# A four-layer kernel on one core: the bias wait, the projection's PSUM bank, the split of the maxima, and identity products at two places

## The reference

```python
x = x + _layernorm(_L0_attn_ref(_layernorm(x), Wqkv, bqkv, Wout, bout))
x = x + _layernorm(_L0_ffn_ref(_layernorm(x), ...))    # two-level Kronecker experts, top 2 of 64
x = x + _layernorm(_L1_attn_ref(_layernorm(x), ...))   # gated state-space layer
x = x + _layernorm(_L1_ffn_ref(_layernorm(x), ...))    # soft mixture of 64 experts, 32 slots each
```

```python
scores = einsum('bhid,bhjd->bhij', q, k) * scale
band = abs(idx[:, None] - idx[None, :]) <= 64
attn = softmax(where(band, scores, neg), axis=-1)
out = einsum('bhij,bhjd->bhid', attn, v).reshape(b, n, d) @ Wout + bout
```

## Time and profile before

| | us |
|---|---|
| median of 3 runs | 841.96 (840.02 to 847.08) |
| the profiled execution | 849.46 |
| its span in the trace | 847.4 |
| PE busy | 665.3 (79%) |
| DVE busy | 488.3 (58%) |
| ACT busy | 362.7 (43%) |
| POOL busy | 332.2 (39%) |
| PE clock granted, mean | 0.889 |

### The profile page before, as it was taken

One profiled execution on the slowest core, in us unless ns is written; L12 is line 12 of the kernel. 1 busy time (PEld: TensorE's weight loads), 2 busy tenths in 40 slices (PEclk: granted clock), 3 DMA queues, 4 the chain that ended last, 5 costly groups with the idle time before them and its releaser, 6 DMA issues. The chain is left out here.

```text
span 847.4 us, 17741 instructions
## 1 busy us (share of the span) xinstructions
PE 665.3 (79%) x7348; PEld 380.4 (45%) x7348; DVE 488.3 (58%) x1088; ACT 362.7 (43%) x626; POOL 332.2 (39%) x324
## 2 busy tenths in 40 slices
PE   4618888888878389968974687079998988999995
PEld 2302444444444289867874334033333344444442
DVE  6505566666654533343315576969999973505255
ACT  3500455555555653342424752265445536424320
POOL 3000444444445200000002344129989964965530
PEclk9955999999995569987987799579999999999998
DMA  4555300000000554000000820000000000000000
GB/s 85 84 80 70 65 3 3 3 3 3 3 3 1 211 105 101 4 3 2 4 5 11 332 39 1 0 0 0 1 0 1 1 0 2 0 1 2 12 12 25
DMA packets 16659, 27.16 MB, mean 32 GB/s; under 512 B 3507, under 2 KB 13684, under 8 KB 15556
## 3 DMA queue, kind: packets, MB, share of 16 engines
q1 hardware_dynamic: 15662, 25.82, 13.2%
q10 hardware_dynamic: 918, 0.21, 0.1%
HBM read 18.11 MB, written 1.05 MB: 23 GB/s over the span
## 5 line engine op out<-in xcount | busy, mean ns | idle before, releaser
L348 DVE TENSOR_REDUCE at_neg_max<-at_psum 128x2 f32<-128x512 f32 x136 | 89.5, 686 | 70.2 <-PE at_psum L586 65.6
L304 POOL TENSOR_SCALAR_AFFINE_SELECT at_exp<-at_exp 128x512 f32<-128x512 f32 x68 | 45.4, 668 | 179.2 <-ACT at_exp L489 179.1
L489 ACT ACTIVATE at_exp<-at_psum 128x512 f32<-128x512 f32 x136 | 80.8, 602 | 80.8 <-PE at_psum L599 79.0
L1559 POOL TENSOR_TENSOR all_phi_b<-all_phi_b,mo_work 128x512 f32<-128x512 f32 x56 | 71.1, 1269 | 43.3 <-ACT mo_work L1765 38.6
L580 PE MATMUL at_psum<-at_mask,all_ident_bf 128*128 128x512 bf16 x136 | 56.1, 413 | 31.4 <-issue 20.1
L1580 PE MATMUL all_psum<-all_phi,mo_xt 128*128 128x512 f32 x128 | 67.1, 651 | 7.3 <-ACT mo_work L1747 5.6
L815 POOL TENSOR_TENSOR all_x<-all_x,ff_x_blocks 128x512 f32<-128x512 f32 x3 | 3.9, 1291 | 171.2 <-ACT ff_x_blocks L1006 171.2
L1529 POOL TENSOR_TENSOR mo_work<-mo_work,mo_max 128x1024 f32<-128x1024 f32 x32 | 61.2, 1912 | 22.1 <-DVE mo_max L1821 22.1
L1613 PE MATMUL all_psum<-mo_xt,all_phi_centred 128*128 128x512 f32 x128 | 65.4, 591 | 0.0
L1666 PE MATMUL all_psum<-mo_work,mo_y_slots 128*128 128x512 f32 x128 | 62.5, 595 | 1.8 <-DVE mo_work L1869 1.8
L1765 ACT ACTIVATE mo_work<-all_psum 128x512 f32<-128x512 f32 x64 | 37.7, 601 | 60.6 <-PE all_psum L1613 60.5
(11 more groups left out here) (341 smaller groups left out, 1294.4 us busy)
## 6 DMA issues: line engine op xcount, KB each, us to landing
all_expert_w<-in_expert_w SPq DMA_DIRECT2D x1, 4096.0 KB, 18.2
ff_b_up<-in_b_up SPq DMA_DIRECT2D x1, 2048.0 KB, 9.7
ff_a_up<-in_a_up SPq DMA_DIRECT2D x1, 2048.0 KB, 18.9
ff_w_down<-in_w_down SPq DMA_DIRECT2D x2, 1024.0 KB, 21.4
ff_b_up<-in_b_down SPq DMA_DIRECT2D x2, 512.0 KB
ff_b_up<-in_a_down SPq DMA_DIRECT2D x2, 512.0 KB
all_phi<-in_phi SPq DMA_DIRECT2D x1, 1024.0 KB, 7.3
all_phi_b<-in_phi_b SPq DMA_DIRECT2D x1, 1024.0 KB, 9.3
```

Of the source, the lines that this page charges most:

```text
L348: v.tensor_reduce(nm[:, r, 0, j:j + 2], psum[:, SN + n % 3, :].rearrange("p (i k) -> p i k", i=2), AX_X, ALU.max, negate=True).then_inc(sn ...
L489: nc.scalar.activation(e[:, m // 2, 2 * (m % 2):2 * (m % 2) + 2, :, :].rearrange("p h j q -> p (h j q)"), psum[:, ST + n % 3, :], ACT.Exp, ...
L1559: nc.gpsimd.tensor_tensor(tot[:, ch % 2, :], first, ec[:, ch % 2, j, :], ALU.add).then_inc(added, 1)
```

## The change

- **Bias.** The wait for `bias_in` moves from ahead of the first mask product to the first projection, `project(0)` in step 3.
- **Projection.** It writes columns 128 to 255 of bank MISC in place of one of the three rotating banks, and moves from behind unit 1 to behind unit 3 of a step. `values_nat` waits for `y_ready`, since it overwrites these columns; it moves from behind unit 4 to behind unit 5. `attn_t` moves from behind unit 6 to behind unit 7, `take_attn` to unit 0 of the next step, `take_y` from unit 2 to 3.
- **Maxima.** `nm` is doubled; VectorE waits for the turning of the window before the last. The two subtractions go to GpSimd, behind the selects of window w for the maxima of window w + 2.
- **Identity products.** In steps 15 and 16, which have no natural scores, one 512-column identity product stands ahead of each unit. In `kmoe` there are 13 at the stage's start, 3 behind the second and the fourth group of transposes, and 8 and 3 ahead of the two waits of `route`, which runs twice.

```diff
-        nm = a.sb("neg_max", [P, 2, 3, NP])
+        nm = a.sb("neg_max", [P, 2, 2, 3, NP])
         def nat_unit(w, m):
-            s = w - 2
-            return NU * w + m + max(0, s - 3) + (1 if s >= 3 and m >= 2 else 0)
+            return NU * w + m
...
+                def parts(w):
+                    g.wait_ge(sn_free, NU * w + NU)
+                    t = nm[:, w % 2]
+                    high = lambda k: t[:, :, k, :].bitcast(BF16).rearrange("p r (h b) -> p r h b", b=2)[:, :, :, 1]
+                    nc.gpsimd.tensor_tensor(t[:, :, 1, :], t[:, :, 0, :], high(0), ALU.subtract).then_inc(nch, 1)
+                    g.wait_ge(nch, 2 * w + 1)
+                    nc.gpsimd.tensor_tensor(t[:, :, 2, :], t[:, :, 1, :], high(1), ALU.subtract).then_inc(nch, 1)
...
+                    if w + 2 < NW:
+                        parts(w + 2)
...
-                    if m == 0 and w >= 1:
-                        dve.wait_ge(mt_done, w)
+                    if m == 0 and w >= 2:
+                        dve.wait_ge(mt_done, w - 1)
...
-                        if m == 1 and s >= 3:
+                        if m == 7 and s >= 3:
                             with_bias(s - 3)
...
-                        if m == 2 and s >= 3:
+                        if m == 3 and s >= 3:
                             take_y(s - 3)
-                        if m == 6 and s >= 1:
-                            take_attn(s - 1)
+                        if m == 0 and s >= 2:
+                            take_attn(s - 2)
...
                     if s + 2 < NW:
                         open_natural(s + 2, m)
+                    else:
+                        pe.wait_ge(sn_free, NU * NW)
+                        keep_warm(1, SN + m % 3)
...
                 def values_nat(w):
+                    if w >= 2:
+                        pe.wait_ge(y_ready, w - 1)
...
                 def project(t):
-                    n = proj_unit(t)
-                    slot_free(pe, n)
                     pe.wait_ge(at_ready, t + 2)
+                    pe.wait_ge(mt_ready, min(t + 5, NW))
+                    if t == 0:
+                        pe.wait_ge(bias_in, 16)
...
-                pe.wait_ge(bias_in, 16)
                 pe.wait_ge(pv_zeroed, 1)
...
-                        if m == 1 and s >= 3:
+                        if m == 3 and s >= 3:
                             project(s - 3)
-                        if m == 4 and s >= 1:
+                        if m == 5 and s >= 1:
                             values_nat(s - 1)
-                        if m == 6 and s >= 1:
+                        if m == 7 and s >= 1:
                             attn_t(s - 1)
...
+                keep_warm(13)
                 for ch in range(4):
...
+                    if ch % 2 == 1:
+                        keep_warm(3)
...
                     for kind in range(2):
+                        keep_warm((8, 3)[kind])
                         pe.wait_ge(oh_ready, 2 * n + kind + 1)
```

More of the change, by code:

```diff
@@ L223, in nat_unit @@
         def nat_unit(w, m):
-            s = w - 2
-            return NU * w + m + max(0, s - 3) + (1 if s >= 3 and m >= 2 else 0)
-        def proj_unit(t):
-            return min(NU * (t + 5) + 2, NU * NW) + t
-        proj_at = {proj_unit(t): t for t in range(NT)}
-        def slot_free(pe, n):
-            if n < 3:
-                return
-            if n - 3 in proj_at:
-                pe.wait_ge(y_ready, proj_at[n - 3] + 1)
-            else:
-                pe.wait_ge(sn_free, n - 2 - sum(k <= n - 3 for k in proj_at))
+            return NU * w + m
         with nc.Block() as block:
@@ L511, in take_y @@
                 def take_y(t):
-                    n = proj_unit(t)
-                    act.wait_ge(sn_done, n + 1)
-                    nc.scalar.copy(y[:, t, :], psum[:, SN + n % 3, 0:P]).then_inc(y_ready, 1)
+                    act.wait_ge(proj_done, t + 1)
+                    nc.scalar.copy(y[:, t, :], psum[:, MISC, P:2 * P]).then_inc(y_ready, 1)
                 take_maxima(0)
@@ L541, in _, with keep_warm @@
             def _(pe):
-                def keep_warm(n):
+                def keep_warm(n, bank=5):
                     for _ in range(n):
-                        nc.tensor.matmul(psum[:, 5, :].rearrange("p (k n) -> p k n", k=4), c["identb"][:, :], c["identb"][:, :].unsqueeze(1).broadcast_to([P, 4, P]), start=True, stop=True)
+                        nc.tensor.matmul(psum[:, bank, :].rearrange("p (k n) -> p k n", k=4), c["identb"][:, :], c["identb"][:, :].unsqueeze(1).broadcast_to([P, 4, P]), start=True, stop=True)
                 def transposes(ch):
@@ L578, in open_natural @@
                                 pe.wait_ge(stacked[ch], 16 * 24)
-                    slot_free(pe, n)
+                    if n >= 3:
+                        pe.wait_ge(sn_free, n - 2)
                     nc.tensor.matmul(psum[:, SN + n % 3, :].rearrange("p (i k) -> p i k", i=2), c["identb"][:, :], mask[:, :].unsqueeze(1).broadcast_to([P, 2, 2 * P]), start=True, stop=False)
@@ L649, in project @@
                 def project(t):
-                    n = proj_unit(t)
-                    slot_free(pe, n)
                     pe.wait_ge(at_ready, t + 2)
+                    pe.wait_ge(mt_ready, min(t + 5, NW))
+                    if t == 0:
+                        pe.wait_ge(bias_in, 16)
                     col = 64 + P * t
-                    nc.tensor.matmul(psum[:, SN + n % 3, 0:P], ones[:, 0:P], bias_rows[:, :], start=True, stop=False)
-                    nc.tensor.matmul(psum[:, SN + n % 3, 0:P], a_t[:, col:col + P], wout[:, :], start=False, stop=True).then_inc(sn_done, 1)
+                    nc.tensor.matmul(psum[:, MISC, P:2 * P], ones[:, 0:P], bias_rows[:, :], start=True, stop=False)
+                    nc.tensor.matmul(psum[:, MISC, P:2 * P], a_t[:, col:col + P], wout[:, :], start=False, stop=True).then_inc(proj_done, 1)
                 pe.wait_ge(ident_loaded, 16)
@@ L1021, in _, with keep_warm @@
                 t_ = nc.tensor
+                def keep_warm(n):
+                    for _ in range(n):
+                        t_.matmul(psum[:, 7, :].rearrange("p (k n) -> p k n", k=4), c["identb"][:, :], c["identb"][:, :].unsqueeze(1).broadcast_to([P, 4, P]), start=True, stop=True)
+                keep_warm(13)
                 for ch in range(4):
```

17 lines of the change are left out of this document (6 added, 11 removed).

## The result

The changed kernel takes **809.27 us** (803.95 to 816.35); the forecast was 816. Its ratio to the kernel before is 0.9585, 95% interval 0.9502 to 0.9667. The profiled execution took 806.43 us with a span of 804.7 (before: 849.46 and 847.4); the granted clock is 0.917 in the mean (0.889).

What follows compares the result with a forecast made beforehand. It took TensorE's bias wait and its loop waits as the bound, with DMA bounding the first 100 us after the change. 12.2 + 7.9 + 3.5 + 2 = 25.6 us off the 841.96 median gave 816 us; range 798 to 840.

Steps and rivals of the forecast that it cites:

- The sum: Whole kernel: 12.2 us from the start, 7.9 loop, 3.5 loop's end and 2 expert stage make 25.6 us saved.
- The first product and the first stretch: Windows 0 and 1: first mask product at 41.2 instead of 61.13; stretch 16.3 us instead of 20.4.
- The new wait: Step 2: turned maxima's transfer lands 13.3 us after issue, TensorE stands still 7 us, leaving a 12.2 us lead.
- rival A: Step 2: the transfer comes in time, no new wait, the lead stays at 24: 799 us; chance 13%.
- How long the clock stays down: Loop: one step more at half clock after step 2, then 11 steps at 9.95 us: +7.9 us.
- The -4.2 of the sum: Loop: cost in us of the one further half-clock step after step 2, 15.2 against 11.04.
- Rivals B: Loop: half clock for 2 to 5 steps behind step 2, 5.3 us per further one: 821 to 837 us; chance 16%.
- rival C: Loop, steps 3 to 14: the clock does not come back, about 885 us, slower; chance 14%.
- Steps of the loop: Loop at full clock: 9.26 us of work plus a 0.7 us wait, 9.95 a step, 1.1 less.
- rival D: Loop: GpSimd's subtractions cost over 0.85 us each, so the steps give nothing: 829 us; chance 5%.
- End of the loop: Steps 15 and 16 stay at full clock with identity products: 23.5 us in place of 27.0, so 3.5 saved.
- Expert stage: Expert stage routings: products ahead of the first one-hot cost 1.0, line 1048 saves 2.1, second routing about 1; together 2 us.

Runs made afterwards that it cites:

- e10: The kernel before the change, run again unchanged for a second trace: 841.95 us.
- e3: The changed kernel run again unchanged, for the spread of its start: 809.85 us, ratio to before 0.9627.
- e4: The changed kernel without any of its new identity products, at the loop's end and in the expert stage: 816.93 us, ratio to before 0.9619.
- e1: The kernel before with one edit, the bias wait moved to the first projection: 832.14 us, ratio to before 0.9878.
- e6: The changed kernel with the two subtractions back on VectorE, nm still doubled: 811.56 us, ratio to before 0.9692.
- e7: The changed kernel without the expert stage's identity products, those of steps 15 and 16 kept: 816.95 us, ratio to before 0.9690.
- e5: The kernel before with only nm doubled and the two subtractions on GpSimd: 850.20 us, ratio to before 1.0113.
- e8: x1 with the subtractions on VectorE and one nm for all windows: 802.91 us, ratio to before 0.9538.
- x1: The changed kernel with stack group 2's transfers metered, at most three under way: 805.31 us, ratio to before 0.9602.
- e9: x1 without any of the new identity products: 807.68 us, ratio to before 0.9583.
- x2: x1 with the split on VectorE, two nm, and 10 identity products in place of 24 ahead of step 0: 804.57 us, ratio 0.9535.

## Why the prediction was right, and where its steps were not

The time, 809.27, lies in the range and in the forecast's own (806 to 828). The sum had 25.6 us. Its parts are best judged with two ordinary traces, e10 and e3, whose spans differ by 33.6: the start gave 112.63 - 96.99 = 15.6, the loop 132.61 - 112.95 = 19.7, the rest -1.7. The sum had 12.2, 7.9 and 5.5. It came out near because terms too small and a term too large partly cancelled, which is luck. The rest can't be judged from two traces at all: it lies between 594.7 and 600.4 in the 14 of them, with no order by kernel.

*The first product and the first stretch.* Right: 40.83 (41.2 foreseen), and 57.70 - 40.83 = 16.9 us (16.3) with the clock falling in it (0.62 in the mean from 44 on). The stretch of before was 20.0 and not 20.4, since its second turning begins at 81.15, so it gave 3.1 us and not 4. Wrong was to take 61.13 for the place of before: e10 has 53.48. The gain of 19.9 is a number of one execution (12.7 against e10); a transfer's landing in a full queue can't be read off a single trace.

*The new wait.* Right in its mechanism, which six traces with the bias moved show at the predicted place: 1.31, 2.43, 3.00, 3.26, 6.76 and 6.89 us, 8.2 to 14.4 us from the issue to the product where I had 13.3. The error was one number for what is a spread. In the first trace rival A's case came nearly true (1.31 us, no fall of the clock, a lead of 23.9); in e4 the forecast's. Of the rule of the Trainium skill ("DMA: Bandwidth & Descriptors", queues, rings and completion order), that each DMA engine changes between the queue rows after every packet, I wrote that by it there would be no new wait. The traces agree once the small transfer has begun: from then on packets of both queues move in the same microseconds (9 to 14 beside 31 to 44 each from 81 to 85 us, before). They go against what I concluded: with the same instruction on ScalarE's own row, the first packet came 5.2 to 10.0 us after the issue with the bulk unmetered, and within 1.4 with three transfers in flight. The row of its own does not protect a small transfer from a backlog here; in which part of the chip it stands meanwhile is not shown.

*How long the clock stays down.* I took step 2 and one more at half clock, and priced steps of 15.2 us. In e1 and e4 the turning of step 3 already stood 13.0 to 13.7 us behind that of step 2, and the 12 steps after it ran at 1.00 throughout. Rivals B and C found no support: work of this mix lifted the clock again after 15.7 us in e1, 13.1 in e4, and 5 in e6 and e7. With waits of 1.31, 2.43, 3.26 and 6.76 us (first trace, e3, e6, e7) the turning of step 3 came 9.3 to 9.8 us behind that of step 2, so no whole step ran at half clock. The -4.2 of the sum had no step to stand for. The fall of step 1 was not foreseen: in e1, e3, e4, e6 and e7 TensorE waited 1.38 to 2.93 us ahead of that step too, and its clock was down for 3 to 7 us in it. What decides between 3 us and 16 is not shown; the length of the wait alone does not (6.76 in e7, 6.89 in e4). The Trainium skill ("TensorE: Matmul & The Clock Gate", "HAM oscillation") was the ground for rival C; the first half of it, a fall after a wait for a transfer, agrees with e1, e4, e6 and e7, but not every such wait did it: 1.31 us in the first trace and 2.43 in e3 left the clock of step 2 at 1.00.

*Steps of the loop.* 1.64 us each in place of 1.1, over 12 steps in place of 11: with the point above, this is the term that was most mis-sized (19.7 for 7.9). Two sizes failed. GpSimd's subtraction takes 0.21 us, not 0.3 (the line through 128 and 512 elements overstated 16), and the wait ahead of the turning is 0.47, not 0.7. And the kernel's own work is 9.41 - 0.47 = 8.94, not the 9.26 that I got by taking the printed waits off the period. Busy time in the windows fell from 110.5 to 106.2 us for the same products, whose busy time by line is unchanged. I take this to be overlap of pipelined products, which a wait breaks; an estimate from it is 0.12 us for each wait beyond what its bracket says (4.3 us over 12 steps with 3 waits fewer). The other kernels fit it: an ordinary step less its printed waits is 9.27 us with four waits (before), 9.11 with three (e5), 8.92 and 8.86 with one (after, e8).

The attribution of 0.30 to the doubled nm failed too: in e5 that wait is gone and the next one is longer by 0.36 a step; in e8 it is absent with one nm. And rival D, in the small, is real: the split on GpSimd costs 0.16 to 0.2 us a step where VectorE would hide it.

*End of the loop* (3.5 foreseen, 0 measured). The step that failed is "with identity products, steps 15 and 16 stay at full clock", from which a shorter time was concluded. They did, mostly (0.89 in place of 0.53), and the stretch took 27.4 us in place of 27.0. I had counted ScalarE's exponentials and left out the chain that ends last: VectorE's norm and additions, the select beside them, the last values. From the start of the additions to the end of the stretch it takes 9.1 us in place of 10.3, but the additions begin 18.3 us behind the turning of step 15 in place of 16.7.

*Expert stage* (2 foreseen). The first routing's 8 products took 3.6 us (3.4 foreseen), but the dense products that then started at full clock soon stood still. TensorE's timeline, after:

```profile
257.77 3.62 PE L1020 MATMUL ff_psum<-all_ident_bf 128*128 128x512 bf16 x8
261.18 0.63 PE L1044 MATMUL ff_psum<-all_ident,ff_one_hot 128*128 128x128 f32 x2
...
262.80 3.71 PE L1052 MATMUL ff_psum<-ff_one_hot_t,ff_b_up 128*64 128x128 f32 x64
268.00 1.20 PE L1052 MATMUL ff_psum<-ff_one_hot_t,ff_b_up 128*64 128x128 f32 x18 [1.48 <-ACT ff_b_taken L954]
```

64 of them in 3.71 us (0.058 each, against 0.105 at half clock in the earlier trace rows), and then a wait for ScalarE's copy. 1.4 us of the 2 were seen in the comparison of x1 and e9.

## What to carry to other kernels

Look, before placing an early start, at which small transfers will then meet a full queue, and meter the bulk that nobody needs yet: here that took the spread from 12 us to 3 and, by medians of runs that were not timed together, 4 us off the time. Read a landing time in a full queue from two traces at least. Test the parts of a bundled change apart: here one of them (the projection's own bank, with the steps moved for it) carried the loop's whole gain, one (the second buffer) nothing, and one (the split on GpSimd) was a loss that the bundle hid.

## What the hardware did that I had not expected

- DMA of the same transfers, in the same stretch from 27 to 41 us, ran at 80 to 83 GB/s in six traces and at 101 to 103 in seven (94 in x2), of the same kernel and of different ones.
- A pair of 6 KB transfers on ScalarE's queue moved its first packet when SyncE's queue had moved 0.64 to 0.75 MB of 128 KB transfers (5.2 to 10.0 us, ten traces), and within 1.4 us with three of them in flight (four traces).
- A GpSimd select of 128 x 512, 0.63 us elsewhere, took 1.8 to 3.0 us while VectorE ran 12 additions of 128 x 128, and ended 0.5 us behind them in each of seven traces.
- After a wait of 3.0 to 6.9 us ahead of step 2 the clock came back with 5 us of the loop's work (e6, e7) or only with 13.1 and 15.7 (e4, e1), though it hadn't come back in the sparser first stretch.
